# A macaron transformer block on one core: entry by one sequence, clamps moved to GpSimd, a new order of the steps

## What is computed

```python
x = x + 0.5 * ffn(layernorm(x))    # ffn: two layers of local attention and a gated GELU network
x = x + attn(layernorm(x))         # 16 heads of 8 channels, causal
x = x + 0.5 * ffn(layernorm(x))

# one of the two layers in ffn
q, k, v = split(shift_token(x) @ wqkv)              # 8 heads of 64
q, k = l2norm(q) * qs, l2norm(k) * ksc              # norm clipped at 1e-12
q, k = rotary_xpos(q, k)
x = x + local_attention(q, k, v) @ wo               # windows of 64, look at one before
h = layernorm(shift_token(x)) * lg + lb             # variance + 1e-5 under the root
a, g = split(h @ w1 + b1)
x = x + (a * gelu(g)) @ w2 + b2
```

## Time and profile before

| | us |
|---|---|
| median of 3 runs (2004.87 to 2005.1) | 2004.96 |
| the profiled execution | 2005.93 |
| its span, first to last instruction | 2004.1 |
| one round of four sequences, 904.25 to 1385.49 | 481.24 |

### The profile page before, as it was taken

One profiled execution on the slowest core, in us unless ns is written; L12 is line 12 of the kernel. 1 busy time (PEld: TensorE's weight loads), 2 busy tenths in 40 slices (PEclk: granted clock), 3 DMA queues, 4 the chain that ended last, 5 costly groups with the idle time before them and its releaser, 6 DMA issues.

```text
span 2004.1 us, 48536 instructions
## 1 busy us (share of the span) xinstructions
PE 1722.5 (86%) x17528; PEld 1353.8 (68%) x17528; DVE 1670.6 (83%) x3487; ACT 1584.0 (79%) x4960; POOL 1202.8 (60%) x1162
## 2 busy tenths in 40 slices
PE   3688999898788899888888889988878889988986
PEld 2477776677667676677766777667766767666775
DVE  6688887888888887888899887888988897888884
ACT  2468897878786899888877789888868778988874
POOL 7677304687678801577788850366767791066870
PEclk7799998999999999999999999999999999999998
DMA  3100000010110000000011000000100010000000
GB/s 100 25 20 12 10 1 17 10 23 20 25 28 20 18 1 3 15 18 18 23 33 25 18 9 1 9 17 17 23 17 23 17 26 2 1 17 18 18 18 11
DMA packets 31686, 36.29 MB, mean 18 GB/s; under 512 B 7986, under 2 KB 18652, under 8 KB 31452
## 3 DMA queue, kind: packets, MB, share of 16 engines
q1 hardware_dynamic: 31452, 33.19, 7.2%
HBM read 5.91 MB, written 2.10 MB: 4 GB/s over the span
## 4 chain that ended last, share of the span: by engine, by line
DVE 36%; ACT 28%; PE 17%; issue 10%; POOL 9%; DMA 0%; ACTq 0%; POOLq 0%; DVEq 0%
ACT probs L885 13%; DVE parts L1152 10%; PE ps_pool L1224 5%; DVE sums L1157 5%; DVE probs L1073 5%; ACT turned L903 4%; POOL rnorm L821 3%; DVE neg_max L1060 3%; PE ps_pool L1297 3%; POOL parts L818 3%; POOL roped L827 3%; ACT L885 2%; ACT L950 2%; DVE sums_floor L1160 2%; PE ps_pool L1368 2%
## 5 line engine op out<-in xcount | busy, mean ns | idle before, releaser
L885 ACT ACTIVATE probs<-ps_scores,neg_max 128x128 f32<-128x128 f32 (+1 forms) x1536 | 577.5, 412 | 71.6 <-DVE neg_max L1060 70.0
L818 POOL TENSOR_TENSOR parts<-parts 128x256 f32<-128x256 f32 x512 | 392.1, 787 | 331.1 <-DVE parts L1152 331.1
L821 POOL TENSOR_TENSOR rnorm<-sums_floor,neg_half 128x8 f32<-128x8 f32 x256 | 440.3, 1720 | 0.0
L885 ACT ACTIVATION_READ_ACCUMULATOR probs<-ps_scores,neg_max 128x1 f32 x1536 | 358.5, 234 | 0.0
L1152 DVE TENSOR_TENSOR parts<-ps_pool,rope 128x1024 f32<-128x1024 f32 x256 | 311.5, 1217 | 38.6 <-ACT squares L931 33.0
L806 POOL TENSOR_TENSOR rstd<-var_eps,neg_half 128x2 f32<-128x2 f32 x112 | 82.0, 732 | 416.8 <-DVE var_eps L1088 413.6
L1060 DVE TENSOR_REDUCE neg_max<-ps_scores 128x4 f32<-128x512 f32 (+1 forms) x448 | 295.4, 682 | 27.5 <-PE ps_scores L1265 16.7
L827 POOL TENSOR_TENSOR roped<-parts,rnorm 128x512 f32<-128x512 f32 x256 | 294.9, 1152 | 37.2 <-POOL rnorm L821 0.9
L1297 PE MATMUL ps_pool<-ident,probs 128*128 128x128 f32 x1792 | 265.7, 286 | 56.0 <-DVE probs L1073 34.8
L903 ACT ACTIVATE turned<-ps_pool 128x512 f32<-128x512 f32 x448 | 255.6, 617 | 63.9 <-PE ps_pool L1297 62.9
L1073 DVE TENSOR_TENSOR probs<-probs,prob_inv 128x1024 f32<-128x1024 f32 (+1 forms) x256 | 293.2, 1166 | 6.6
(11 more groups left out here) (114 smaller groups left out, 3725.7 us busy)
## 6 DMA issues: line engine op xcount, KB each, us to landing
between<-val SPq DMA_DIRECT2D x192, 128.0 KB, 2.2
x_in<-in_L_attn_x_dram SPq DMA_DIRECT2D x16, 128.0 KB, 2.3
out_dram<-x_sb SPq DMA_DIRECT2D x16, 128.0 KB, 1.8
stage<-in_L_ffn_wqkv_dram SPq DMA_DIRECT2D x2, 768.0 KB, 5.4
stage<-in_L_ffn_w_dram SPq DMA_DIRECT2D x2, 341.0 KB
wo<-in_L_ffn_wo_dram SPq DMA_DIRECT2D x2, 256.0 KB
rope_in<-in_rope_dram SPq DMA_DIRECT2D x1, 256.0 KB, 2.9
w<-in_L_ffn_w_dram SPq DMA_DIRECT2D x2, 128.0 KB
```

The lines of the kernel that those rows point to most:

```text
L818: last = nc.gpsimd.tensor_tensor(joined[:, :, dst], joined[:, :, dst], sines[:, :, src], ALU.add)
L821: nc.gpsimd.tensor_tensor(rnorm[:, u], sums_floor[:, u], neg_half[:], ALU.pow).then_inc(sems["pool_step"], 1)
L885: last = nc.scalar.activation(probs[:, u, block:block + wide].rearrange("p b j -> p (b j)"), bank[:, at:at + P * wide], ACT.Exp, bias=neg_ ...
```

## The change

1. `EARLY` is 1: only sequence 0 does its entry ahead of the weights. What was left of the preparation behind the fifth rope follows the fourth directly.
2. The clamp of the sums of squares and the addition of epsilon move from VectorE to GpSimd, and the memset ahead of the latter goes. GpSimd waits for its own small instruction before it takes the power.
3. The turns of attention are written out as a list. In the first round it starts staggered, with sequence 0 taking its second turn before sequence 3 its first; the later rounds go around as before.
4. The planner's prices, handovers (now with 0.1 more where TensorE is the receiver) and due times have other values, so all lists are laid out anew.
5. The buffer `gelu` is the buffer `hidden`; the multiplication is done in place.

```diff
-EARLY = 2
+EARLY = 1
...
-    "W1": [(PE, 0.75), (ACTE, 0.36), (DVE, 0.4)], "W2": [(PE, 1.32), (DVE, 0.97)], "WOF": [(PE, 1.76), (DVE, 0.45)],
+    "W1": [(PE, 0.71), (ACTE, 0.36), (DVE, 0.4)], "W2": [(PE, 1.31), (DVE, 0.9)], "WOF": [(PE, 1.73), (DVE, 0.4)],
...
-HANDOVER = (0.21, 0.19, 0.16, 0.12)
+HANDOVER = (0.2, 0.16, 0.12, 0.08)
+WEIGHTS = 0.1
...
+def handover(by, to):
+    return 0.0 if by == to else HANDOVER[by] + (WEIGHTS if to == PE else 0.0)
...
-TURNS = sorted(((s, ph) for s in range(SEQS) for ph in range(1, LEAVE, 2)),
-               key=lambda x: (x[0] // STREAMS * LEAVE + x[1] + STAGGER[x[0] % STREAMS], x[0] % STREAMS))
+TURNS_OF = [0, 1, 2, 0, 3, 1, 2, 0, 3, 1, 2, 3, 0, 1, 2, 3, 0, 1, 2, 3, 4, 5, 6, 7, 4, 5, 6, 7, 4, 5, 6, 7, 4, 5, 6,
...
-        gelu = sb("gelu", [P, HC, T])
-        hidden = sb("hidden", [P, HC, T])
+        gelu = hidden = sb("hidden", [P, HC, T])
...
                 pool.wait_ge(sems["var_ready"], count("var_ready", step))
+                nc.gpsimd.tensor_scalar(var_eps[s][:], mean_var[s][:, :, 1], EPS, None, ALU.add).then_inc(sems["pool_step"], 1)
+                pool.wait_ge(sems["pool_step"], count("pool_step", step))
                 nc.gpsimd.tensor_tensor(rstd[s][:], var_eps[s][:], neg_half[:, 0:TILES], ALU.pow).then_inc(sems["rstd_ready"], 1)
...
                 pool.wait_ge(sems["squares_summed"], count("squares_summed", step))
+                nc.gpsimd.tensor_scalar(sums_floor[:, u], sums[:, u], NORM_FLOOR * NORM_FLOOR, None,
+                                        ALU.max).then_inc(sems["pool_step"], 1)
+                pool.wait_ge(sems["pool_step"], count("pool_step", step, 1))
                 nc.gpsimd.tensor_tensor(rnorm[:, u], sums_floor[:, u], neg_half[:], ALU.pow).then_inc(sems["pool_step"], 1)
...
-                nc.vector.memset(var_eps[s][:], 0.0)
                 for t in range(TILES):
                     last = nc.vector.bn_aggr(mean_var[s][:, t], bn[s][:, t])
-                last.then_inc(sems["vector_step"], 1)
-                dve.wait_ge(sems["vector_step"], count("vector_step", step))
-                nc.vector.tensor_scalar(var_eps[s][:], mean_var[s][:, :, 1], EPS, None, ALU.add).then_inc(sems["var_ready"], 1)
+                last.then_inc(sems["var_ready"], 1)
...
                     nc.vector.tensor_reduce(sums[:, u], squares[:, square].rearrange("p (h d) -> p h d", d=LOCAL_D), AX,
-                                            ALU.add).then_inc(sems["vector_step"], 1)
-                    dve.wait_ge(sems["vector_step"], count("vector_step", step))
-                    nc.vector.tensor_scalar(sums_floor[:, u], sums[:, u], NORM_FLOOR * NORM_FLOOR, None,
-                                            ALU.max).then_inc(sems["squares_summed"], 1)
+                                            ALU.add).then_inc(sems["squares_summed"], 1)
...
+            for part in range(projections - 1, 4):
+                prepare(part)
             prepare_biases()
```

## The result

The changed kernel takes 1945.8 us, the median of 4 runs (1944.86 to 1947.52), against 2005.03 before: a ratio of 0.9694, interval 0.9663 to 0.9724. It is 59 us faster; the forecast was 40. The profiled execution took 1947.52 with a span of 1945.7.

What follows compares the result with a forecast made beforehand. No engine was taken as full; the time lay in work and handovers between engines. Opening -11, clamps -17, order -10 and end -2 summed to -40 us from 2004.96, giving 1965, range 1925 to 1999.

Steps and rivals of the forecast that it cites:

- The start and the opening: Sequence 1's entry leaves the preparation: main part starts about 26.5 us earlier, 11 us of it gained by the twenty-fourth rope.
- most of this is not gained: Opening: of the 26.5 us earlier start, only 14 us by VectorE's ledger or 11 by GpSimd's are gained.
- My end of -19: Opening: the most favourable bound on the gain from the earlier entry, 19 us; the other bound was a 5 us loss.
- The clamps: Rounds: moving clamp and epsilon to GpSimd relieves VectorE by 25 us a round, adds 43 to GpSimd, nets -17 us.
- the 31 by full durations: Rounds: VectorE's relief in us a round if the small instructions' full durations and preceding idle time went; 25 was taken instead.
- the estimate by shares of the chain: Rounds: each engine's change counts by its chain share, VectorE 36%, GpSimd 9%: net gain 4.2 us a round, 17 in four.
- the first rival: Rounds: VectorE's relief passes on more fully, half of 25 us a round, GpSimd's longer step hides: about 1925 us; chance 0.18.
- my ends (0 and -50): Rounds: bounds for moving the clamps, from nothing (TensorE sets the pace) to half of 25 us a round, 50 in four.
- The third rival: Ropes: GpSimd becomes pacer, kernel slower, about 2030 us, from a quarter of the chain in the rounds; chance 0.12.
- The order: Rounds: newly laid lists work on TensorE's 57 idle us, gaining 2.5 us a round, 10 in all; ends -32 and +24.
- The end: Last sequence: its values move ahead of the other's gated network, 3.4 us earlier, statistics give back about one: -2 us.
- the buffer in place: Gated network: using hidden as gelu adds no wait, since one VectorE instruction reads and writes the same elements: nothing.

Runs made afterwards that it cites:

- C alone: Kernel before with only the clamp and epsilon moved from VectorE to GpSimd, lists unchanged: 2091.63 us, ratio 1.0439.
- C and E: Kernel before with clamp and epsilon moved to GpSimd and entry by one sequence, old turns, prices and due times: 2153.4 us, ratio 1.0729.
- O alone: Kernel before with only the new turns, prices, handovers and due times, entry by two sequences, clamps on VectorE: 2012.65 us, ratio 1.0043.

## Why the prediction came out as it did

Direction and range were right, by a sum whose terms were not.

- **The start and the opening (-11).** The ledger to the twenty-fourth rope was right: the first matmul at 49.16 (48 forecast), that rope's end at 161.6 (160), 9.5 us gained. (Its 1.13 us for L1152 stands in no line of the earlier trace rows; the trace has it, from 1129.12 to 1130.25.) But I let the opening stand for the whole effect. Undone by itself, the entry is worth 35 us, all in the first round. The failed step is "most of this is not gained, since sequence 1's entry has to be done later": it holds at the twenty-fourth rope, where 13.2 of 27.5 are left, and by the end of the first round nothing has been given back. My end of -19 was not wide enough. In the old lists, with their other first and second round, the same step costs 54: the size belongs to the lists as much as to the entry.
- **The clamps (-17).** VectorE's part was sized nearly right: it lost 20.4 us a round by C alone, 18.6 in the new lists and 23.6 where both steps were gone from the old ones, for 25 forecast (the 31 by full durations is further off). GpSimd's was too large: it gained 31 us a round, for 43, since a clamp puts 0.32 us between starts and not 0.5. What failed is the estimate by shares of the chain, 10.5 us saved and 6.3 added a round. In the new lists the move gives 34 us, about 12 in the second and third rounds each, which is the price of the first rival (half of the 25 us); in the old lists it costs 86. The first lies within my ends (0 and -50), the second far outside. A share tells who is last now, and nothing of how close the next one is: with GpSimd's steps as long as before to about 1%, its share quadrupled once VectorE was relieved.
- **The third rival's decision point** fell with it. I had the kernel turn slower from the point where GpSimd carries a quarter of the chain. It carries 26% in the changed kernel, which is 3% faster, and 27% in the one with sorted turns, which is 4% slower: the share does not decide.
- **The order (-10), "the weakest term".** By itself it is +7, and in the steady rounds nothing clear without C (481.0 and 481.6 against 480.8 and 481.2). With C and E it is worth 208. It is not a term of its own. The fault is that I priced C and E as if they were laid into lists that stay, and O as if it worked on a kernel without them.
- **The end (-2) and the buffer in place (0).** The last back projection and the other sequence's gated network stand as forecast:

```profile
1925.22 1.97 PE L1364 MATMUL ps_pool<-q_t,wo 128*128 128x256 f32 x8 [0.20 <-ACT q_t L934]
1926.84 0.47 PE L1240 MATMUL ps_pool<-h_hi,w_hi 128*128 128x256 f32 x1
```

  The last round gains 10.2 us: 6.7 are there with the clamps still on VectorE (453.6 for 460.3), and 7.6 with O alone (452.7). So the new order gives about 7 in the last round, where I had 2.5 for the order and 2 for the end; how much of it is this one exchange no run separates. The buffer in place, at nothing, was not tried by itself; no run shows that term.

One way through the four kernels that adds up is: the order (2005 to 2013), then the entry (to 1980), then the clamps (to 1946). Taken the other way, clamps first, then the entry, then the order, the same change reads +86, +62, -208. Even by the first way, the kinder one, my -40 came near the -59 by luck, since errors offset one another: the entry (-33 there) too small by 22, the clamps (-34) by 17, and order and end (+8 for -12) too good by 20.

## What to carry to other kernels

In a kernel whose queues are written at build time, durations and order are one thing: an edit that changes a step's engine has to be tried in more than one order, and an edit that loses in the old lists has not been shown bad (here +86 became -34). A layout with the new prices alone is not enough for that (2105 us here); the turns and due times counted too. To price such an edit, look beside the chain at the engine that is next: whether the receiver's waits would grow if the present last one were quicker; taking the step away from both engines is the cheapest experiment that shows it. And a step that can be removed, as by a column that carries the floor, is worth more than one that is moved (-14 us here).

## What the runs showed of the hardware

Two things that I had not expected. Some of GpSimd's steps are much longer where VectorE runs long instructions between buffers in on-chip memory beside them. In the preparation of the changed kernel, GpSimd's timeline reads

```profile
33.57 3.63 POOL L835 TENSOR_TENSOR parts<-parts 128x256 f32<-128x256 f32 x2
...
39.50 2.39 POOL L847 TENSOR_TENSOR roped<-parts,rnorm 128x512 f32<-128x512 f32 x1
```

where the same steps take 1.43 and 1.04 us elsewhere. VectorE works on the weights beside them:

```profile
34.47 2.17 DVE L1039 TENSOR_TENSOR wqkv_lo<-stage,wqkv_hi 128x1536 fp32r<-128x1536 f32 x1
...
37.75 1.57 DVE L1043 TENSOR_TENSOR w_lo<-scaled,w_hi 128x1364 fp32r<-128x1364 f32 x1
39.24 1.75 DVE L1044 TENSOR_TENSOR wf_lo<-padded,wf_hi 128x1536 fp32r<-128x1536 f32 x1
```

The first step is longer by 2.2 us, as much as L1039 lasts, and the second by 1.35. But the power that ran beside L1043, from 37.68, took its usual 1.68 us, so not every overlap costs. No run here took VectorE's work away from beside them, so that it is the cause is argued and not shown.

And the variants in which the time is longest have the lowest granted clock of TensorE: 0.971 of 2.4 GHz in the mean of the changed kernel, 0.963 before, 0.945 with C alone and 0.936 with C and E. The mean mixes stretches at 2.4 and at 1.2 GHz. In the second round of C alone TensorE was busy for 437.3 us at 0.95, against 423.9 at 0.98 before, with as many matmuls: 13.4 us more work and 7.6 more idle time make the 21 by which the round is longer. The third round of C alone is as long (501.1), with 433.2 us busy at 0.97. So up to 4 us of slower work in one round did not reach its end, and how much of the rest did, no run here separates.
